# Keys as three products, values first, and a first load in slices, in a two-layer cross-attention and feed-forward kernel

## The chip, the cores and the metric

One core of one Trainium2 chip. The metric is the device time of one execution in microseconds, lower is better. The kernel keeps all five engines at work: TensorE (PE, matmuls), VectorE (DVE), ScalarE (ACT), GpSimd (POOL) and SyncE (SP, which issues the DMAs here). Each runs its own list of instructions in the written order; semaphores hold an instruction until others are done.

## The reference, cut to what matters

`x` has 2 x 256 rows of 512, `ctx_4096` 2 x 512 rows of 512. Everything is float32 at the boundary.

```python
x = x + xattn0(layernorm(x), ctx)     # 8-bit fake quantisation of both, then q1 @ q2
x = x + ffn0(layernorm(x))            # weights to fp4, rows to fp6, per block of 32; silu(gate) * up, down
x = x + xattn1(layernorm(x), ctx)     # 32 query heads, 8 key/value heads of 128, rope, softmax, wo
x = x + ffn1(layernorm(x))            # ternary weights with scales, inner width 1376
```

In `xattn1` the keys are `ctx @ wk` and the values `ctx @ wv`, both 1024 x 1024. They depend on the context alone, so they can be computed at any time before it. The change is about when and how they are computed.

## The kernel before

**Stages.** Stage one, 0 to about 122 us, does several things at once: the first layernorm and the quantised attention `xattn0`; the quantisation to fp4 and transposition of the weights of `ffn0` (8 chunks of four 128x512 tiles and a last single tile); and the projection of values and keys for `xattn1`. Stage two, 122 to 177 us, is `ffn0` for four tiles of 128 rows. Then follow `xattn1`, a loop over 32 heads (to about 600 us), and `ffn1`.

**Units.** A unit is one PSUM bank of 128x512: `("v", i, h)` is context tile i (0 to 7) times half h of `wv`; `("k", i, b)` is key head i for batch b. A float32 unit is four slices of the contraction, which the profile shows as eight matmuls. `STEPS` (line 40) gives for each of the eight steps the units before and after the first half of the chunk's transposes; five key units (`LATE_KEYS`) are worked off in stage two. Units rotate over banks 5, 6, 7; `take` waits until ScalarE has copied out the unit three places earlier. The sums of `xattn0` (in steps 3 and 4) and the transposes of q1 use the same banks.

**A weight chunk.** `mx_peaks` (VectorE, block maxima, 1339) and `mx_exponents` (two tensor_scalars, 1345 and 1347, giving `mx_e` and `mx_r`); `scale_in` (GpSimd, 1104); `mx_lift` (ScalarE, two halves, 882); `mx_round` (VectorE, 1357, 1360); `mx_clip` (VectorE, 1365); `scale_out` (GpSimd, 1110, giving `mx_w`); `mx_turn` (TensorE, two times eight transposes, 514); `mx_keep` (ScalarE, 874). The lists of all engines are written out by hand, two chunks apart: GpSimd does scale_in(i+2), then scale_out(i). `fp6_out` (GpSimd, 1115) is the last part of the quantisation of rows; VectorE's part of it is `fp6` and `fp6_clip` (1370 to 1382): a reduction, four small tensor_scalars, a multiply, a small tensor_scalar and a clip.

**Keys of head 0.** They don't go to the scratch memory as they are: ScalarE's `swap` copies them and their halves exchanged, GpSimd's `key_rotate` does three 128x512 tensor_tensors (rope), and SyncE stores the result. This is done for both batches near the start, from 27 and 41 us.

**SyncE's order.** wk of head 0, context columns of batch 0 (1 MB), x (1 MB), scalars, wv half 0, weight chunks 0 and 1, identity, context columns of batch 1, rope table, wv half 1, chunk 2, and so on. `three` (lines 663 to 665), used by the later stages, computes one product of operands that are split in a high and a low part (float32r) as high x high + high x low + low x high.

## Time and profile before

| | us |
|---|---|
| median of 3 runs | 702.56 (700.72 to 702.59) |
| the profiled execution | 702.53 |
| its span in the trace | 700.7 |
| TensorE busy | 668.3 (95%) |
| VectorE busy | 520.0 (74%) |
| GpSimd busy | 463.3 (66%) |
| ScalarE busy | 363.3 (52%) |

A timeline row gives start and length in us from the span's start, the engine, the line, what is written from what, and in brackets how long the engine sat idle before it and who ended that. A row of the chain says what the execution was waiting for at that time, followed back from the last instruction; `issue` is time in which the engine at hand waited for nothing that the profile shows. Matmul lengths include the tail of the last one, so back-to-back groups overlap by a little.

### The profile page before, as it was taken

The numbers are of one execution on the slowest core, as the hardware profiler recorded it, in microseconds if no ns is written. First come the engines' busy times: TensorE is split into PE (matmuls) and PEld (weight loads), VectorE is DVE, ScalarE is ACT, GpSimd is POOL, SyncE is SP. The second block draws the span as 40 slices with busy tenths as digits, with TensorE's granted clock in tenths as the row PEclk, the third lists the DMA queues.
The fourth block names the chain that finished last, engine by engine and source line by source line (L and its number), as shares of the span: only waits on it lengthen the run. The fifth ranks groups of instructions, "written<-read, shape, count | busy, mean of one in ns | idle before, by whom it ended". The sixth has DMA issues, their size and how long they took to land.

```text
span 700.7 us, 11095 instructions
## 1 busy us (share of the span) xinstructions
PE 668.3 (95%) x3152; PEld 494.0 (70%) x3152; DVE 520.0 (74%) x1046; ACT 363.3 (52%) x686; POOL 463.3 (66%) x407
## 2 busy tenths in 40 slices
PE   6999998899899999999999999999999999799997
PEld 2444443444577788888888888888888877688885
DVE  4999798777668888888888888888888886721122
ACT  2697434533565665666666665665665663211110
POOL 0697426432479878778789788688698478066661
PEclk9999999999999999999999999999999999999999
DMA  9985422140323132141131221221223012013311
GB/s 340 343 293 183 134 87 80 36 155 6 127 71 119 30 106 76 30 134 45 55 110 45 82 83 45 90 75 46 89 75 135 17 31 66 25 46 101 113 56 61
DMA packets 39420, 67.27 MB, mean 96 GB/s; under 512 B 3680, under 2 KB 12000, under 8 KB 38368
## 3 DMA queue, kind: packets, MB, share of 16 engines
q1 hardware_dynamic: 39392, 66.93, 28.9%
q8 instruction: 14, 0.23, 0.1%
q14 instruction: 14, 0.11, 0.1%
HBM read 57.48 MB, written 9.44 MB: 95 GB/s over the span
## 4 chain that ended last, share of the span: by engine, by line
PE 71%; POOL 10%; DVE 8%; issue 7%; ACT 2%; DMA 1%; SPq 0%; POOLq 0%; DVEq 0%; ACTq 0%
PE ps L663 16%; PE ps L665 16%; PE ps L664 16%; PE ps L731 11%; PE ps L696 7%; POOL mx_raw L1104 3%; POOL mx_w L1110 3%; PE ps L584 2%; PE ps L520 1%; DMA X<-in_x 1%; PE ps L536 1%; POOL prob L1161 1%; PE ps L620 1%; DVE mx_amax L1339 1%; DVE stats L1260 1%
## 5 line engine op out<-in xcount | busy, mean ns | idle before, releaser
L1009 ACT ACTIVATE prob<-ps,nmax 128x512 f32<-128x512 f32 x128 | 88.3, 690 | 97.4 <-DVE nmax L1487 97.0
L1161 POOL TENSOR_SCALAR prob<-prob,rinv 128x512 f32<-128x512 f32 x128 | 89.4, 698 | 73.7 <-DVE rinv L1494 73.6
L731 PE MATMUL ps<-xt,wq_sb 128*128 128x512 f32 x384 | 103.2, 393 | 3.8 <-DVE q_cos L1502 2.1
L1020 ACT CAST pT<-ps 128x512 fp32r<-128x512 f32 x128 | 75.1, 587 | 52.8 <-PE ps L696 51.9
L1487 DVE CUSTOM_DVE_ANT_0 ps<-ps,mask_sb 128x512 f32<-128x512 f32 x128 | 87.9, 687 | 6.7 <-PE ps L665 6.3
L1508 DVE TENSOR_TENSOR pT<-ps,pT 128x512 fp32r<-128x512 f32 x128 | 86.3, 674 | 3.0 <-ACT pT L1020 2.0
L731 PEld LDWEIGHTS ps<-xt,wq_sb 128*128 128x128 f32 x384 | 71.6, 188 | 22.0 <-issue 4.6
L696 PE MATMUL ps<-idf,prob 128*128 128x128 f32 x512 | 76.7, 272 | 0.4 <-POOL prob L1161 0.3
L696 PEld LDWEIGHTS ps<-idf,prob 128*128 128x128 f32 x512 | 63.8, 141 | 17.3 <-POOL prob L1161 1.6
L520 PE MATMUL ps<-ctxT,wk_sb 128*128 128x512 f32 x128 | 60.5, 613 | 6.5 <-DMA ctxT<-in_ctx_cols 6.5
L1104 POOL TENSOR_TENSOR mx_raw<-mx_raw,mx_r 128x2048 f32<-128x2048 f32 (+1 forms) x9 | 30.2, 3354 | 53.7 <-DVE mx_r L1347 53.7
L663 PE MATMUL ps<-pT,vt 128*128 128x512 f32 x128 | 61.1, 478 | 0.5 <-DVE pT L1508 0.5
L536 PE MATMUL ps<-wv_sb,ctxT 128*128 128x512 f32 x128 | 57.3, 597 | 0.6 <-ACT v_st L869 0.4
L1164 POOL TENSOR_TENSOR q_swp<-q_swp,ropeQ 128x512 f32<-128x512 f32 x32 | 47.0, 1469 | 10.9 <-ACT q_swp L1030 10.9
L663 PE MATMUL ps<-wo_sb,oT 128*128 128x512 f32 x128 | 50.3, 393 | 1.4 <-DVE X L1543 0.9
L663 PE MATMUL ps<-kt,qt 128*128 128x512 f32 x128 | 50.6, 395 | 0.9 <-DVE kt L1521 0.5
L1561 DVE SCALAR_TENSOR_TENSOR int<-ps,sc,silu 128x512 f32<-128x512 f32 x11 | 8.3, 750 | 57.6 <-PE ps L665 57.6
L665 PE MATMUL ps<-pT,vt 128*128 128x512 f32 x128 | 50.8, 397 | 0.0
L664 PE MATMUL ps<-pT,vt 128*128 128x512 f32 x128 | 50.3, 393 | 0.0
L665 PE MATMUL ps<-kt,qt 128*128 128x512 f32 x128 | 50.1, 392 | 0.0
L1145 POOL TENSOR_TENSOR wo_sb<-wo_raw,wo_sb 128x512 fp32r<-128x512 f32 x32 | 48.3, 1511 | 2.7
L664 PE MATMUL ps<-wo_sb,oT 128*128 128x512 f32 x128 | 50.0, 391 | 0.0
(177 smaller groups left out, 1587.9 us busy)
## 6 DMA issues: line engine op xcount, KB each, us to landing
mx_raw<-in_mxw SPq DMA_DIRECT2D x8, 1024.0 KB, 5.5
wq_raw<-in_wq SPq DMA_DIRECT2D x32, 256.0 KB, 3.2
wo_raw<-in_wo SPq DMA_DIRECT2D x32, 256.0 KB, 2.7
v_scr<-v_st SPq DMA_DIRECT2D x16, 256.0 KB, 2.5
kr<-k_scr SPq DMA_DIRECT2D x16, 256.0 KB, 2.9
vr<-v_scr SPq DMA_DIRECT2D x16, 256.0 KB, 3.4
k_scr<-k_st SPq DMA_DIRECT2D x14, 256.0 KB, 2.1
kr_swp<-k_scr SPq DMA_DIRECT2D x28, 128.0 KB, 3.3
```

The source lines that it names most:

```text
L520: last = mm(bank(n), wk_sb[:, i % 2, k], ctxT[:, k, b * CTX:(b + 1) * CTX], start=(k == 0), stop=(k == KD - 1))
L536: last = mm(bank(n), ctxT[:, k, i * P:(i + 1) * P], wv_sb[:, k, h * 512:(h + 1) * 512], start=(k == 0), stop=(k == KD - 1))
L663: mm(out_ap, left[0], right[0], start=first, stop=False)
L664: mm(out_ap, left[0], right[1], start=False, stop=False)
L665: return mm(out_ap, left[1], right[0], start=False, stop=final)
L696: last = nc.tensor.transpose(bank(2 + i % 2)[:, k * P:(k + 1) * P], prob[:, i, k * P:(k + 1) * P], idf[:])
L731: last = mm(query_bank(H), wq_sb[:, par, l, k], xt[:, r, k], start=(n == 0), stop=(n == 11))
L1009: nc.scalar.activation(prob[:, j], bank(j % 2), ACT.Exp, bias=nmax[:, j:j + 1], scale=-1.0, accum_out=rsum[:, j:j + 1]).then_inc(exps, 1)
L1020: copy(pT[:, v % 2, 0, :, i * P:(i + 1) * P], bank(2 + i % 2).rearrange("p (k c) -> p k c", k=4)).then_inc(ph_ready, 1)
L1161: nc.gpsimd.tensor_scalar(prob[:, i], prob[:, i], rinv[:, i:i + 1], 1.0, ALU.mult, ALU.mult).then_inc(probs, 1)
L1487: nc.vector.tensor_tensor_reduce(out=bank(j % 2), in0=bank(j % 2), in1=mask_sb[:, 2 * (u % 2) + j % 2], scale=-1.0, scalar=BIG, op0=ALU.ad ...
L1508: tt(pT[:, v % 2, 1, :, i * P:(i + 1) * P], bank(2 + i % 2).rearrange("p (k c) -> p k c", k=4), pT[:, v % 2, 0, :, i * P:(i + 1) * P].bitc ...
```

## The change

Values come first and keys last in stage one. The first four value units run together, slice by slice, on banks 0, 5, 6 and 7, as the slices of context and wv (256 KB each) arrive; two pairs of slices are loaded ahead of x and two behind it, all ahead of the first weight chunk. Keys are computed with `three`: context and key weights are split in a high part (ScalarE's copy to float32r: `context_high`, `weights_high`) and a low part (GpSimd's subtraction: `context_low`, `weights_low`). The high part of the context overwrites wv, the low part overwrites the context, so both wait for the value units that read them. Key weights have four slots; slots 2 and 3 lie in the staging buffer of the values, and their loads wait for the value stores. Head 0 is third among the key heads, so `key_rotate` moves to the ends of GpSimd's steps 5 and 6. `mx_r` moves from VectorE to GpSimd (`exponents`). ScalarE's first instructions are reordered. The buffers of the attention stage and of the last net are laid out in another order, with the same sizes.

```diff
...
 STEPS = (
-    ([("v", 0, 0), ("v", 1, 0), ("v", 2, 0), ("v", 3, 0)], [("k", 0, 1)]),
-    ([("v", 0, 1), ("v", 1, 1), ("k", 1, 0)], [("k", 1, 1)]),
-    ([("v", 2, 1), ("k", 2, 0)], [("v", 3, 1)]),
-    ([("k", 2, 1), ("v", 4, 0)], [("v", 4, 1)]),
-    ([("k", 3, 0), ("k", 3, 1)], [("v", 5, 0)]),
-    ([("v", 5, 1), ("k", 4, 0)], [("k", 4, 1)]),
-    ([("v", 6, 0), ("v", 6, 1)], [("v", 7, 0)]),
-    ([("v", 7, 1), ("k", 5, 0)], []),
+    ([("v", 0, 0), ("v", 1, 0), ("v", 2, 0), ("v", 3, 0)], [("v", 4, 0)]),
+    ([("v", 5, 0), ("v", 6, 0), ("v", 7, 0)], [("v", 0, 1)]),
+    ([("v", 1, 1), ("v", 2, 1)], [("v", 3, 1)]),
+    ([("v", 4, 1), ("v", 5, 1)], [("v", 6, 1)]),
+    ([("v", 7, 1), ("k", 1, 0)], [("k", 2, 0)]),
+    ([("k", 1, 1), ("k", 2, 1)], [("k", 0, 0)]),
+    ([("k", 0, 1), ("k", 3, 0)], [("k", 3, 1)]),
+    ([("k", 4, 0), ("k", 4, 1), ("k", 5, 0)], []),
 )
 LATE_KEYS = ((5, 1), (6, 0), (6, 1), (7, 0), (7, 1))
 LATE_BANK = (3, 6, 2, 1, 3)
 VALUES = [unit[1:] for step in STEPS for part in step for unit in part if unit[0] == "v"]
-KEYS_AT = {1: 2, 2: 3, 4: 4, 5: 5}
+KEYS = [unit[1:] for step in STEPS for part in step for unit in part if unit[0] == "k"] + list(LATE_KEYS)
+STORED_KEYS = [key for key in KEYS if key[0] > 0]
+HEADS = [head for head, batch in KEYS if batch == 0]
 Q_AT, L0_AT = 1, 4
+V_LAST = 4
+
+HIGH_AT = {V_LAST - 1: (0, 1), V_LAST: (2, 3), V_LAST + 1: (4, 5), V_LAST + 2: (6,)}
...
         for i in range(NFULL):
-            rotation += STEPS[i][0] + STEPS[i][1]
+            rotation += STEPS[i][0][1 if i == 0 else 0:] + STEPS[i][1]
...
 
+            if unit == ("v", 0, 0):
+                return 0
...
+        def wk_parts(i):
+
+            turn = HEADS.index(i)
+            raw, high, low = (wk_01, wk_hi01, wk_lo01) if turn % 4 < 2 else (wk_23, wk_hi23, wk_lo23)
+            return raw[:, turn % 2], high[:, turn % 2], low[:, turn % 2]
...
             def k_load(i):
 
-                after(sp, k_sums, 2 * (i - 1))
-                sp.dma_start(wk_sb[:, i % 2], wk[i]).then_inc(wk_in[i % 2], 16)
+                turn = HEADS.index(i)
+                if turn >= 4:
+                    sp.wait_ge(*keys_summed(HEADS[turn - 4], 1))
+                sp.dma_start(wk_parts(i)[0], wk[i]).then_inc(wk_in[turn % 4], 16)
 
...
+            def slice_load(k):
+                sp.dma_start(ctxT[:, k, 0:CTX], ctx_cols[k * P:(k + 1) * P, 0:CTX]).then_inc(ctxT0_in[k], 16)
+                sp.dma_start(wv_sb[:, k, 0:512], wv[k * P:(k + 1) * P, 0:512]).then_inc(wv0_in[k], 16)
...
-            k_load(0)
-            ctxT_load(0)
+            slice_load(0)
+            slice_load(1)
             sp.dma_start(X[:], x.rearrange("(t p) d -> p t d", p=P)).then_inc(x_in, 16)
             sp.dma_start(sc[:], scalars).then_inc(sc_in, 16)
-            wv_load(0)
+            slice_load(2)
+            slice_load(3)
             mx_load(0)
             mx_load(1)
             sp.dma_start(idf[:], ident).then_inc(id_in, 16)
-            ctxT_load(1)
-            sp.dma_start(ropeK[:], rope_k).then_inc(rk_in, 16)
-            wv_load(1)
+            sp.dma_start(ctxT[:, :, CTX:CTOK], ctx_cols[:, CTX:CTOK].rearrange("(k p) c -> p k c", p=P)).then_inc(ctxT1_in, 16)
             mx_load(2)
-            k_load(1)
             ctx_load(0)
+            sp.dma_start(wv_sb[:, :, 512:1024], wv[:, 512:1024].rearrange("(k p) c -> p k c", p=P)).then_inc(wv1_in, 16)
             stores(STEPS[0][0])
             mx_load(NRAW)
             ctx_load(1)
+            k_load(HEADS[0])
+            k_load(HEADS[1])
+            sp.dma_start(ropeK[:], rope_k).then_inc(rk_in, 16)
+            stores(STEPS[0][1])
             for i in range(1, NFULL):
-                if i in KEYS_AT:
-                    k_load(KEYS_AT[i])
                 if i + NRAW <= NFULL:
                     mx_load(i + NRAW)
-                if i == 1:
-                    for b in range(2):
-                        sp.wait_ge(k_roped, b + 1)
-                        sp.dma_start(k_scr[0, b], k_own[:, b]).then_inc(k0_stored, 16)
-                stores(STEPS[i][0] + STEPS[i][1])
-            k_load(6)
+                if i > V_LAST:
+                    k_load(HEADS[4 if i == V_LAST + 1 else i])
+                if i == V_LAST + 1:
+                    k_load(HEADS[5])
+                units = [unit for part in STEPS[i] for unit in part if unit[:2] != ("k", 0)]
+                if i == V_LAST:
+                    stores(units[:1])
+                    for slot in range(NSLOT):
+                        sp.wait_ge(v_stored[slot], 16 * 2 * NCT // NSLOT)
+                    k_load(HEADS[2])
+                    k_load(HEADS[3])
+                    units = units[1:]
+                stores(units)
+            for b in range(2):
+                sp.wait_ge(k_roped, b + 1)
+                sp.dma_start(k_scr[0, b], k_own[:, b]).then_inc(k0_stored, 16)
 
...
+            def three(out_ap, left, right, first, final):
+
+                mm(out_ap, left[0], right[0], start=first, stop=False)
+                mm(out_ap, left[0], right[1], start=False, stop=False)
+                return mm(out_ap, left[1], right[0], start=False, stop=final)
+
             def key_part(i, b, n, parts):
+                pe.wait_ge(wk_split, HEADS.index(i) + 1)
+                _, high, low = wk_parts(i)
+                cols = slice(b * CTX, (b + 1) * CTX)
                 for k in parts:
-                    last = mm(bank(n), wk_sb[:, i % 2, k], ctxT[:, k, b * CTX:(b + 1) * CTX], start=(k == 0), stop=(k == KD - 1))
+                    if i == HEADS[0] and k % 2 == 0:
+                        pe.wait_ge(ctx_split, 2 * b + k // 2 + 1)
+                    last = three(bank(n), [high[:, k], low[:, k]], [ctx_hi[:, k, cols], ctx_lo[:, k, cols]], k == 0, k == KD - 1)
...
+            def first_values():
+
+                units = STEPS[0][0]
+                for k in range(KD):
+                    pe.wait_ge(ctxT0_in[k], 16)
+                    pe.wait_ge(wv0_in[k], 16)
+                    for unit in units:
+                        i = unit[1]
+                        last = mm(bank(rotating(unit)), ctxT[:, k, i * P:(i + 1) * P], wv_sb[:, k, 0:512], start=(k == 0), stop=(k == KD - 1))
+                        if k == KD - 1:
+                            last.then_inc(v_sums, 1)
...
-            keys(0, 0, 0)
+            first_values()
             for i in range(NFULL):
-                project_context(STEPS[i][0])
+                if i > 0:
+                    project_context(STEPS[i][0])
                 if i == 1:
                     pe.wait_ge(consts_ready, 2)
-                    pe.wait_ge(*keys_out(0, 0))
+                    pe.wait_ge(v_copied, 1)
                 if 0 < i < NFULL - 1:
...
             def swap(b):
 
-                act.wait_ge(k_sums, b + 1)
+                act.wait_ge(*keys_summed(0, b))
...
             def copy_unit(unit):
                 kind, i, j = unit
-                if kind == "k":
+                if kind == "k" and i == 0:
+                    swap(j)
+                elif kind == "k":
                     copy_keys(i, j)
                 else:
                     copy_values(i, j)
 
-            swap(0)
+            def context_high(b):
+
+                act.wait_ge(v_sums, NCT * (b + 1))
+                cols = slice(b * CTX, (b + 1) * CTX)
+                for k in range(0, KD, 2):
+                    copy(ctx_hi[:, k:k + 2, cols], ctxT[:, k:k + 2, cols]).then_inc(ctx_high, 1)
+
+            def weights_high(i):
+                raw, high, _ = wk_parts(i)
+                turn = HEADS.index(i)
+                act.wait_ge(wk_in[turn % 4], 16 * (turn // 4 + 1))
+                copy(high, raw).then_inc(wk_high, 1)
+
+            rows_scale()
+            mx_lift(0, 0)
+            mx_lift(0, 1)
             copy_values(0, 0)
             copy_values(1, 0)
-            mx_lift(0, 0)
-            mx_lift(0, 1)
-            rows_scale()
-            copy_values(2, 0)
             act.wait_ge(id_in, 16)
             copy(idb[:], idf[:]).then_inc(consts_ready, 1)
             mx_lift(1, 0)
+            copy_values(2, 0)
+            mx_lift(1, 1)
             copy_values(3, 0)
-            mx_lift(1, 1)
-            swap(1)
             rows_keep()
+            copy_values(4, 0)
             for i in range(1, NFULL):
                 copy_unit(STEPS[i][0][0])
+                if i == V_LAST:
+                    context_high(1)
                 mx_lift(i + 1, 0)
                 if i == 1:
                     copy_unit(STEPS[i][0][1])
@@ -948,6 +1017,11 @@
                 if i == Q_AT:
                     keep_quantised(0)
                     context_scale(1)
+                if i == V_LAST - 2:
+                    context_high(0)
+                for turn in HIGH_AT.get(i, ()):
+                    weights_high(HEADS[turn])
+            weights_high(HEADS[7])
             keep_quantised(1)
...
+            def exponents(i):
+                n, p = width(i) // BLK, i % NRAW
+                pool.wait_ge(mx_expo, i + 1)
+                ts(mx_r[:, p, 0:n].bitcast(I32), mx_e[:, p, 0:n].bitcast(I32), -1.0, -(2.0 ** 24), ALU.mult, ALU.add).then_inc(mx_scale, 1)
+
             def scale_in(i):
+                exponents(i)
...
+            def context_low(b):
+
+                if b == 0:
+                    pool.wait_ge(v_sums, VALUES.index((3, 1)) + 1)
+                cols = slice(b * CTX, (b + 1) * CTX)
+                for k in range(0, KD, 2):
+                    pool.wait_ge(ctx_high, 2 * b + k // 2 + 1)
+                    tt(ctx_lo[:, k:k + 2, cols], ctxT[:, k:k + 2, cols], ctx_hi[:, k:k + 2, cols].bitcast(F32), ALU.subtract).then_inc(ctx_split, 1)
+
+            def weights_low(i):
+                raw, high, low = wk_parts(i)
+                pool.wait_ge(wk_high, HEADS.index(i) + 1)
+                tt(low, raw, high.bitcast(F32), ALU.subtract).then_inc(wk_split, 1)
+
             scale_in(0)
             scale_in(1)
-            key_rotate(0)
-
             for i in range(NFULL):
                 if i + 2 <= NFULL:
                     scale_in(i + 2)
                 if i == L0_AT + 2:
                     fp6_out(q1[:].rearrange("p t d -> p (t d)"), NT * D, 0, q1_ready)
                 scale_out(i)
-                if i == 0:
-                    key_rotate(1)
+                if i == V_LAST - 2:
+                    context_low(0)
+                for turn in HIGH_AT.get(i, ()):
+                    weights_low(HEADS[turn])
+                if i == V_LAST - 1:
+                    context_low(1)
+                if i in (V_LAST + 1, V_LAST + 2):
+                    key_rotate(i - V_LAST - 1)
+            weights_low(HEADS[7])
             scale_out(NFULL)
...
+            pool.wait_ge(k0_stored, 32)
             for t in range(NT):
...
             def mx_exponents(i):
                 p, m = i % NRAW, width(i) // BLK
                 after(dve, mx_ready, i - NRAW + 1)
-                dve.wait_ge(mxa_step, 2 * i + 1)
-                ts(mx_e[:, p, 0:m].bitcast(U32), mx_amax[:, 0:m].bitcast(U32), EXP_MASK, 0x80000000, ALU.bitwise_and, ALU.bitwise_or).then_inc(mxa_step, 1)
-                dve.wait_ge(mxa_step, 2 * i + 2)
-                ts(mx_r[:, p, 0:m].bitcast(I32), mx_e[:, p, 0:m].bitcast(I32), -1.0, -(2.0 ** 24), ALU.mult, ALU.add).then_inc(mx_scale, 1)
+                dve.wait_ge(mx_peak, i + 1)
+                ts(mx_e[:, p, 0:m].bitcast(U32), mx_amax[:, 0:m].bitcast(U32), EXP_MASK, 0x80000000, ALU.bitwise_and, ALU.bitwise_or).then_inc(mx_expo, 1)
...
```

## Rows read from the trace of the kernel before

**Rows 1.** The page, busy time of the engines: us (share of span), instructions.
```profile
...
PE 668.3 (95%) x3152; PEld 494.0 (70%) x3152; DVE 520.0 (74%) x1046; ACT 363.3 (52%) x686; POOL 463.3 (66%) x407
...
```

**Rows 2.** The chain of waits in order of time: start us, length us, what.
```profile
...
86.99 13.49 issue
...
100.51 3.64 POOL mx_raw L1104
...
104.15 3.60 POOL mx_w L1110
...
107.80 0.62 PE ps L514 x8
...
```

**Rows 3.** TensorE's timeline: start, length, what xcount [idle before it, and its releaser].
```profile
...
6.45 5.71 PE L520 MATMUL ps<-ctxT,wk_sb 128*128 128x512 f32 x8 [6.45 <-DMA ctxT<-in_ctx_cols]
...
12.29 14.00 PE L536 MATMUL ps<-wv_sb,ctxT 128*128 128x512 f32 x32
...
71.55 1.03 PE L499 MATMUL ps<-q,ones 128*128 128x512 bf16 x4
...
107.80 0.62 PE L514 MATMUL ps<-idb,mx_w 128*128 128x128 bf16 x8 [1.49 <-POOL mx_w L1110]
...
119.12 1.06 PE L490 MATMUL ps<-idb,q 128*128 128x128 bf16 x16
...
121.79 4.93 PE L584 MATMUL ps<-WT,q1T 128*128 128x512 bf16 x24 [1.62 <-ACT q1T L839]
...
177.07 5.71 PE L731 MATMUL ps<-xt,wq_sb 128*128 128x512 f32 x24 [1.16 <-DVE xt L1456]
...
```

**Rows 4.** VectorE's timeline, the same columns.
```profile
...
9.52 2.47 DVE L1260 BATCH_NORM_STATS2 stats<-X 128x6 f32<-128x512 f32 x4 [9.52 <-DMA X<-in_x]
...
22.10 1.54 DVE L1345 TENSOR_SCALAR mx_e<-mx_amax 128x64 uint32<-128x64 uint32 x1
...
41.61 1.26 DVE L1345 TENSOR_SCALAR mx_e<-mx_amax 128x64 uint32<-128x64 uint32 x1
...
42.91 1.19 DVE L1347 TENSOR_SCALAR mx_r<-mx_e 128x64 int32<-128x64 int32 x1
...
108.03 0.20 DVE L1371 TENSOR_SCALAR f_amax<-f_amax 128x64 f32<-128x64 f32 x1
...
108.95 2.29 DVE L1375 TENSOR_TENSOR f<-xhat,f_r 128x2048 fp8e4<-128x2048 f32 x1
...
111.38 1.22 DVE L1382 TENSOR_SCALAR f6c<-f 128x2048 bf16<-128x2048 fp8e4 x1
...
129.52 0.68 DVE L1371 TENSOR_SCALAR f_amax<-f_amax 128x44 f32<-128x44 f32 x1
...
136.94 0.56 DVE L1424 TENSOR_TENSOR int<-silu,ps 128x384 f32<-128x384 f32 x1 [2.21 <-ACT silu L958]
...
```

**Rows 5.** ScalarE's groups to 180 us: xcount | busy us, mean ns of one | idle.
```profile
...
L882 ACT ACTIVATE ps<-mx_raw 128x1024 f32<-128x1024 f32 x16 | 16.4, 1030 | 4.3 <-POOL mx_raw L1104 4.3
...
L869 ACT COPY v_st<-ps 128x512 f32<-128x512 f32 x16 | 9.3, 582 | 21.7 <-PE ps L536 21.7
...
```

**Rows 6.** The first key matmuls (line 520), shortest/median/longest duration.
```profile
...
L520 PE MATMUL ps<-ctxT,wk_sb x16: 592/593/1193, 6.5 to 29.1; 128*128 128x512 f32 x16
...
```

**Rows 7.** GpSimd's groups, mean ns of one.
```profile
...
L1145 POOL TENSOR_TENSOR wo_sb<-wo_raw,wo_sb 128x512 fp32r<-128x512 f32 x32 | 48.3, 1511 | 2.7
...
L1225 POOL TENSOR_TENSOR fw_even<-ffn_raw,fw_even 128x1024 fp32r<-128x1024 f32 x5 | 11.9, 2387 | 1.4 <-DVE int1s L1563 1.0
...
L1222 POOL TENSOR_SCALAR fw_even<-ffn_raw 128x512 fp32r<-128x512 f32 x10 | 6.1, 627 | 21.0 <-issue 21.0
...
```

**Rows 8.** GpSimd's timeline.
```profile
...
19.95 3.64 POOL L1104 TENSOR_TENSOR mx_raw<-mx_raw,mx_r 128x2048 f32<-128x2048 f32 x1 [18.99 <-DVE mx_r L1347]
...
41.10 1.72 POOL L1122 TENSOR_TENSOR k_swp<-k_swp,ropeK 128x512 f32<-128x512 f32 x1
...
42.78 1.27 POOL L1123 TENSOR_TENSOR k_own<-k_own,ropeK 128x512 f32<-128x512 f32 x1
...
104.12 3.63 POOL L1110 TENSOR_TENSOR mx_w<-mx_q,mx_e 128x2048 bf16<-128x2048 bf16 x1
...
113.58 1.05 POOL L1104 TENSOR_TENSOR mx_raw<-mx_raw,mx_r 128x512 f32<-128x512 f32 x1 [5.83 <-DVE mx_r L1347]
...
114.58 3.64 POOL L1115 TENSOR_TENSOR q<-f6c,f_e 128x2048 bf16<-128x2048 bf16 x1
...
129.11 1.05 POOL L1110 TENSOR_TENSOR mx_w<-mx_q,mx_e 128x512 bf16<-128x512 bf16 x1 [2.18 <-PE ps L514]
...
```

84 lines of the change are left out of this document (41 added, 43 removed).

## The prediction

> **What bounds the kernel now.** The page comes first: TensorE is busy 95% of the span and GpSimd 66% [rows 1]. That invites "fewer TensorE passes, less time". The chain of waits, read in order of time over the stretch that the change rewrites, says otherwise: from 17 us to 108 us it runs from one GpSimd tensor_tensor to the next, each of 3.64 us, with `issue` pieces between (up to 13.49 us, where GpSimd waits for VectorE's scale), and TensorE enters only at 107.80, after a wait of 1.49 us for GpSimd's `mx_w` [rows 2, 3]. TensorE, VectorE and GpSimd are all close to the limit in this stage, coupled through buffers. So the timelines of the engines must be read side by side, not the busy shares. Behind 121.79 (first gate/up matmul) the same three engines pass the rows of the first feed-forward net around; from 177.07 (first query) the attention loop and the last net follow, which the change leaves as they are.
>
> The views are differenced at two marks: 121.79 and 177.07 [rows 3]. I walked the four written orders and SyncE's forward with the durations of the rows, releasing each instruction when its last wait is met. The present orders, walked so, give 120.4 and 175.0, that is 1.4 and 2.0 us early; the new ones are compared with these, mark by mark, and only differences are used. The sum goes on the profiled execution, 702.53 us (span 700.7 and 1.8 around it), which is the median of the runs (702.56) but for 0.03.
>
> **Start.** Before, key weights and a whole context half (1.25 MB) land at 6.45, and 2.25 MB, with x, at 9.52: 3.07 us per MB [rows 3, 4]. The first pair of slices (0.5 MB) lands by that rate at 6.45 - 0.75 x 3.07 = 4.2; x, now behind 1 MB instead of 1.25, 0.8 earlier at 8.7. The other two pairs follow by 12, before TensorE wants them. First values: 16 slices of work in 4 x 3.44 us (a unit: 14.00/4 less its tail) plus 2.3 us, because the first eight matmuls took 5.71 instead of 3.44: 4.2 + 16.1 = 20.3. Nothing is gained by that: all four units end together and fill banks 0, 5, 6, 7, and v(4,0) needs bank 5. ScalarE now has rows_scale, lift(0,0) and lift(0,1) ahead of the copies. scale_in(0) is done at 16.3 (peaks) + 2.3 + 0.2 + 0.3 (exponents on GpSimd) + 3.64 = 22.7, two lifts and two copies follow, 0.95 and 0.48 each (their 1.03 and 0.58 less the 0.1 by which the next one overlaps) [rows 5]: 25.6. TensorE idles 5.3 us from 20.3.
>
> What that idleness does to its clock: the first matmul, after 6.45 us without work, shows 1193 ns against 592 of the later ones, the lower of the two levels, 1.2 against 2.4 GHz (the column of the granted clock reads 1.00 all the same); after the longest later waits here, 1.6 us, nothing of the sort is seen [rows 3, 6]. 5.3 is nearer to 6.45, so I take the slow start again: 2.2 us on TensorE, between 0 and 2.3. "TensorE: Matmul & The Clock Gate" of the Trainium skill (Part 1, the clock gate) states that an idle engine falls back to half rate; by it the 1.0 us below is owed, without it not.
>
> **26 to 98 us.** At the first attention sums (71.55) TensorE used to have 16 units done, now 15: -2.2 (start) - 3.4 (a unit fewer) + 5.3 (idle) + 2.2 (clock), less what the old waits took: the walk has +0.3. A key unit as three products: 12 matmuls; 24 of that kind take 5.71 us, so 0.23 each and 2.78 per unit instead of 3.44: 0.66 saved, 11 units in the stage 7.3 us, 5 late ones 3.3 us [rows 3]. The additions: ScalarE copies the context's high part in four pieces (0.95 each, as a lift) and eight weight slices (0.52 each, a copy), 8 us, in idle time of 2 to 5 us per step. GpSimd gets four 128x1024 subtractions at 2.39 (9.6 us), eight 128x512 at 1.27 (10.2 us; 1.27 is the rotation's step) and nine exponent operations [rows 7, 8]. No row has a 64-column GpSimd operation of this kind. It lies between 0 and 0.63, the tensor_scalar of 512 columns. Two-source operations of 512 and 2048 columns take 1.05 and 3.64, 1.7 ns per column, and a one-source one I take at half of that: 0.63 - 448 x 0.00085 = 0.25, 2.2 us in all. GpSimd idles 2 us per step early and 13.5 us before 100.51 [rows 2], so 22 us seem to fit.
>
> **The lock.** They don't, for a reason that the timelines show. A VectorE tensor_scalar of 64 columns takes 0.20 us, but 1.54 at 22.10, 1.26 at 41.61, 1.19 at 42.91, 0.68 at 129.52. Each such one ends when the GpSimd operation then running ends: 23.60 against 23.64; 42.82 against 42.87; 44.06 against 44.10; 130.16 against 130.20. Where GpSimd is idle (108.03) it takes 0.20. GpSimd waits in turn: 1.72 instead of 1.27 at 41.10 behind VectorE's clip. Two in a row are each held, since GpSimd's next operation slips in between them [rows 4, 8]. Tensor_reduce and operations with a PSUM source run through unhurt. In the walk a VectorE tensor_scalar from SBUF waits for the running GpSimd operation, and the other way round; this reproduces the present VectorE timeline within 0.5 us up to 65 us. So each added GpSimd operation costs VectorE as much as GpSimd. "GPSIMD Engine Reference" of the Trainium skill (Key points) adds VectorE instructions with two SBUF inputs to those in contention; the 2.29 us multiply of the quantisation (two SBUF inputs) would then be held too, by up to 1.3 us once or twice: 1 to 2 us above my sum. No row here has it beside GpSimd work.
>
> What the products save up to here: l(1) can start 1 us earlier than before, but exponent(6) on VectorE is held by the context subtraction (2.4 us), so the sums are read at the same time, and scale 7 comes with +0.1 (warm clock) or +1.1 (slow start). TensorE's saved time (2 + 5 key units) turns into waiting before the transposes at 107.80: 5.7 us instead of 1.49.
>
> **98 to 122 us.** Behind scale_out(5) (ends 107.75) GpSimd now has two weight subtractions and key_rotate(0), 2 x 1.27 + 3 x 1.27 = 6.3 us, where it had idled till 113.58. Beside them VectorE runs the layernorm output's quantisation: reduce to 108.0, four small tensor_scalars (0.9 us with gaps), the multiply, the clip; done just before chunk 8's scale, which GpSimd gets at 113.58 [rows 4, 8]. Now each of the four is held behind one of the five GpSimd operations: 4 x 1.27 + 0.9 = 6.0 instead of 0.9, +5.0. Then exponents(8), scale_in(8), the 3.64 us product q1, the transposes: +5.0 again, less 0.9 by which TensorE had been the later one at 119.12 (q1 was ready at 114.58 + 3.64 = 118.22): first gate/up +4.2 (warm), +5.3 (slow start).
>
> **122 to 177 us.** Behind q1 GpSimd has scale_out(6) 3.64, a subtraction, key_rotate(1) 3.8, scale_out(7) 3.64, a subtraction, scale_out(8) 1.05: 14.7 us without a pause. VectorE's clips of chunks 7 and 8 are held (+0.6 and +1.2), as is the last rounding by the queue, so its first product comes +6.0; its small tensor_scalars at 129.52 ff. are held by scale_out(7), the last subtraction and scale_out(8): +3.7 more. Of these 2.2 us are lost time it had anyway before 136.94 [rows 4]; chunk 7's transposes come +6.5, in front of gate_up(1). The second quantised tile is +8.6, and from there the loop goes as before, +8.1 at the last transposes of `int_q`. Seven quarters of late key units (1.15 us) then stand on TensorE's way to the last row transposes: +7.0 at the first query (warm), +8.1 (slow start). The late key that is spread over units -2 and -1 saves 0.66, half of it before a wait of 0.46: -0.3. SyncE's key loads wait for sums that come in time; its x, wq and key loads behind the last transposes move with them. Later stages: 0. Sum: 702.5 + 8.0 - 0.3 = 710.2 us.
>
> **Rivals.** (1) The clock stays up through the 5.3 us: 702.5 + 7.0 - 0.3 = 709.2. For: the column reads 1.00. Against: the first matmul. It is inside the forecast's own range. (2) No price of the lock, the other side: if VectorE's small operations fell between GpSimd's (another phase by 1 us at 108 and 130), the walk without holding gives -1.5 at 177.07: TensorE's late keys pay, the stage does not, and 702.5 - 1.5 - 0.3 = 700.7 to 701.5. It decides from the point where the four small tensor_scalars at 108 us take under 1 us. Against it: GpSimd is then busy without gaps for 6 us. Half the holding gives 704 to 706. (3) GpSimd's subtractions take 1.51 us as the `wo` ones do beside VectorE [rows 7]: each 0.24 dearer, the walk gives +2.3: 712.5; with exponent operations of 0.6 us, +0.9 more: 713.4. (4) The change doesn't do what it says: the key units run at 3.44 (weight loads not hidden): +1.5, since only the late ones are on the way: 711.7.
>
> **Chances.** Forecast with (1): 0.60, own range 707.5 to 712; (2) fully 0.13, half 0.12; (3) and (4) together 0.15. The range that leaves out no more than 2 in 10: 702.5 to 713.5. A measurement tells 0.3% (2.1 us) from no change, so same is 700.5 to 704.6: faster 0.09 (the lower half of rival 2 and errors of the walk), same 0.13, slower 0.78.
>
> **What would show it.** Right: TensorE starts near 4.2, idles some 5 us before v(4,0), matmuls at double length after it; a wait of 5 to 6 us ahead of the transposes near 107; four small tensor_scalars near 108 of over 1 us each; the first gate/up at about 126 to 127, the first query at 184 to 186. Wrong: VectorE's small operations at 0.2 us beside GpSimd work, or GpSimd idle between 108 and 138; then the time is near 701. If the first query comes near 177 and the total is off all the same, the moved buffers of the attention stage did it, which I priced at nothing.

## The result, and the profile after

| | before | after |
|---|---|---|
| median of the runs | 702.58 (700.72 to 702.89, 4 runs) | 712.03 (711.31 to 712.56, 4 runs) |
| the profiled execution, its span | 702.53, 700.7 | 711.55, 709.8 |

The ratio is 1.0139, 95% interval 1.0119 to 1.0160: the change costs 9.45 us. The forecast was 710.2, its own range 707.5 to 712, which the measured 712.03 misses by 0.03; the wide range was 702.5 to 713.5.

On the page TensorE is busy for 4.6 us less than in [rows 1], VectorE for 14.3 and GpSimd for 27.5 more:

```profile
...
PE 663.7 (94%) x3211; PEld 508.5 (72%) x3216; DVE 534.3 (75%) x1037; ACT 371.9 (52%) x698; POOL 490.8 (69%) x428
...
```

VectorE has nine instructions fewer, and yet works longer. TensorE's timeline (against [rows 3]; columns as there) shows how late each mark is:

```profile
...
4.64 15.68 PE L589 MATMUL ps<-wv_sb,ctxT 128*128 128x512 f32 x32 [4.64 <-DMA wv_sb<-in_wv]
...
27.65 12.71 PE L599 MATMUL ps<-wv_sb,ctxT 128*128 128x512 f32 x24 [7.32 <-ACT v_st L924]
...
92.03 0.50 PE L566 MATMUL ps<-ctx_hi,wk_hi 128*128 128x512 f32 x1 [3.27 <-DVE col L1423]
...
113.91 1.03 PE L560 MATMUL ps<-idb,mx_w 128*128 128x128 bf16 x8 [5.21 <-POOL mx_w L1190]
...
131.75 6.21 PE L648 MATMUL ps<-WT,q1T 128*128 128x512 bf16 x24 [1.57 <-ACT q1T L896]
...
188.36 5.72 PE L788 MATMUL ps<-xt,wq_sb 128*128 128x512 f32 x24 [1.17 <-DVE xt L1555]
...
```

The transposes of chunk 5 come 6.1 us later (113.91 against 107.80) behind a wait of 5.21 instead of 1.49, the first gate/up 10.0 later, the first query 11.3. From there on nothing is added: the last result of VectorE is 10.8 late. The span ends only 9.1 later, since the last output transfers took 2.5 us behind it in this execution and 4.2 in that of the kernel before. This end comes in two lengths: 2.4 to 2.6 us in eleven of the fourteen traces, 4.2 to 4.6 in three (before, before_extra, keys_whole). So totals of single executions can differ by 1.7 to 2 us for nothing, and the experiments are also compared at VectorE's last result.

VectorE's timeline (against [rows 4]) shows where its 14.3 us are. Between 84 and 123 us it has no gap:

```profile
...
56.55 1.22 DVE L1456 SCALAR_TENSOR_TENSOR mx_raw<-ps,mx_raw 128x1024 f32<-128x1024 bf16 x1 [3.33 <-ACT ps L937]
...
61.34 2.28 DVE L1440 TENSOR_REDUCE mx_amax<-mx_raw 128x64 f32<-128x2048 f32 x1
...
64.66 2.85 DVE L1464 TENSOR_SCALAR mx_q<-mx_q 128x2048 bf16<-128x2048 bf16 x1
67.43 2.34 DVE L1446 TENSOR_SCALAR mx_e<-mx_amax 128x64 uint32<-128x64 uint32 x1
...
93.46 2.91 DVE L1430 SCALAR_TENSOR_TENSOR X<-xhat,sx,X 128x512 f32<-128x512 f32 x2
...
106.01 0.18 DVE L1446 TENSOR_SCALAR mx_e<-mx_amax 128x64 uint32<-128x64 uint32 x1
...
113.80 0.20 DVE L1470 TENSOR_SCALAR f_amax<-f_amax 128x64 f32<-128x64 f32 x1
114.03 1.15 DVE L1471 TENSOR_SCALAR f_amax<-f_amax 128x64 uint32<-128x64 uint32 x1
115.21 1.20 DVE L1472 TENSOR_SCALAR f_r<-f_amax 128x64 int32<-128x64 int32 x1
116.44 1.20 DVE L1473 TENSOR_SCALAR f_r<-f_r 128x64 f32<-128x64 f32 x1
117.68 3.32 DVE L1474 TENSOR_TENSOR f<-xhat,f_r 128x2048 fp8e4<-128x2048 f32 x1
...
```

GpSimd in the same stretch (against [rows 8]):

```profile
...
106.28 0.24 POOL L1178 TENSOR_SCALAR mx_r<-mx_e 128x64 int32<-128x64 int32 x1 [8.77 <-DVE mx_e L1446]
...
113.82 2.54 POOL L1220 TENSOR_TENSOR wk_lo<-wk,wk_hi 128x512 fp32r<-128x512 f32 x2
116.32 1.27 POOL L1202 TENSOR_TENSOR k_swp<-k_swp,ropeK 128x512 f32<-128x512 f32 x1
117.56 1.29 POOL L1203 TENSOR_TENSOR k_own<-k_own,ropeK 128x512 f32<-128x512 f32 x1
118.99 3.16 POOL L1206 TENSOR_TENSOR k_own<-k_own,k_swp 128x512 f32<-128x512 f32 x1
...
```

To be seen: the exponents (64 columns) take 0.18 us at 106.01, where GpSimd is idle, and 2.34 at 67.43, beside a subtraction. The first small instruction starts at 113.80, 0.02 us ahead of GpSimd's subtraction, and takes its 0.20; each of the next three ends within 0.1 us of a GpSimd operation (115.09, 116.36, 117.59). GpSimd waits in turn: its addition at 118.99 takes 3.16 instead of 1.27; the product begun at 117.68 is out at 121.00, and the addition 1.15 later. The row at 61.34 is a mark ahead of the first subtraction (63.66); the kernel before reaches it at 59.58, so 1.8 us of the delay are there already, behind the wait of 3.33 us for ScalarE.

### The profile page after: what moved, and what is told of

It is laid out like the page before. It is cut to its first block, busy times and chain, and to the rows that moved or that the text cites. A ratio compares the mean times of both kernels' runs of the same rounds, so it can differ in the third digit from the quotient of the medians.

```text
span 709.8 us, 11262 instructions
## 1 busy us (share of the span) xinstructions
PE 663.7 (94%) x3211; PEld 508.5 (72%) x3216; DVE 534.3 (75%) x1037; ACT 371.9 (52%) x698; POOL 490.8 (69%) x428
## 4 chain that ended last, share of the span: by engine, by line
PE 69%; DVE 15%; POOL 5%; issue 5%; ACT 3%; DMA 2%; SPq 0%; POOLq 0%; DVEq 0%; ACTq 0%
PE ps L566 16%; PE ps L568 16%; PE ps L567 15%; PE ps L788 11%; PE ps L753 7%; PE ps L648 2%; DVE mx_amax L1440 2%; DVE mx_raw L1456 1%; DVE f L1474 1%; DMA X<-in_x 1%; POOL mx_raw L1184 1%; DMA v_scr<-v_st 1%; DVE f_amax L1469 1%; PE ps L599 1%; DVE stats L1360 1%
## 5 line engine op out<-in xcount | busy, mean ns | idle before, releaser
L599 PE MATMUL ps<-wv_sb,ctxT 128*128 128x512 f32 x96 | 44.9, 620 | 7.3 <-ACT v_st L924 7.3
L566 PE MATMUL ps<-wo_sb,oT 128*128 128x512 f32 x128 | 50.2, 393 | 1.4 <-DVE X L1642 0.9
L566 PE MATMUL ps<-kt,qt 128*128 128x512 f32 x128 | 50.1, 392 | 0.9 <-DVE kt L1620 0.5
L568 PE MATMUL ps<-kt,qt 128*128 128x512 f32 x128 | 50.2, 392 | 0.0
L567 PE MATMUL ps<-wo_sb,oT 128*128 128x512 f32 x128 | 50.0, 391 | 0.0
L568 PE MATMUL ps<-wo_sb,oT 128*128 128x512 f32 x128 | 50.0, 390 | 0.0
L567 PE MATMUL ps<-kt,qt 128*128 128x512 f32 x128 | 49.9, 390 | 0.0
```

The source lines that it names most:

```text
L566: mm(out_ap, left[0], right[0], start=first, stop=False)
L567: mm(out_ap, left[0], right[1], start=False, stop=False)
L568: return mm(out_ap, left[1], right[0], start=False, stop=final)
L599: last = mm(bank(n), ctxT[:, k, i * P:(i + 1) * P], wv_sb[:, k, h * 512:(h + 1) * 512], start=(k == 0), stop=(k == KD - 1))
```

## The experiments

Times are medians; the ratio is to the kernel before on the same chip, with its 95% interval. The marks are of the profiled execution: the exponents of chunk 7 (VectorE), the end of the FP6 chain's last instruction (`f6c`), the first gate/up and the first query (TensorE), and the end of VectorE's last result.

Two things limit what the differences say. The experiments ran on three chips, where the median of the kernel before was 702.46 (no_lows, rotate_late, keys_whole, before_extra), 702.44 (start, norm_late, before_six, before_fp6_first) and 701.16 (no_early_lows, no_late_lows, keep_busy, before_early_last); the changed kernel was not run again beside them. And kernels whose orders are the same up to there reach VectorE's reduction of chunk 4 at anything from 47.95 (keep_busy) to 49.61 (norm_late), 48.84 in the changed kernel, so that a mark further on which moved by less than 1.7 us need not have been moved by the edit.

| kernel | us | ratio | expon. 7 | `f6c` ends | gate/up | query | last result |
|---|---|---|---|---|---|---|---|
| before | 702.5 | | 100.02 | 112.60 | 121.79 | 177.07 | 696.47 |
| after | 712.03 | 1.0119 to 1.0160 | 106.01 | 123.34 | 131.75 | 188.36 | 707.26 |
| no_lows | 705.77 | 1.0036 to 1.0069 | 101.26 | 116.53 | 126.94 | 182.10 | 701.08 |
| no_early_lows | 708.13 | 1.0066 to 1.0124 | 100.83 | 118.16 | 126.56 | 183.14 | 703.64 |
| no_late_lows | 709.92 | 1.0093 to 1.0143 | 106.33 | 121.61 | 131.32 | 186.49 | 705.56 |
| keys_whole | 708.23 | 1.0065 to 1.0119 | 102.14 | 117.39 | 127.46 | 182.73 | 701.73 |
| rotate_late | 718.12 | 1.0203 to 1.0257 | 106.23 | 120.55 | 130.93 | 195.07 | 713.75 |
| start | 711.86 | 1.0106 to 1.0165 | 105.02 | 122.36 | 130.78 | 187.43 | 707.60 |
| norm_late | 717.08 | 1.0181 to 1.0236 | 99.90 | 128.84 | 138.14 | 194.07 | 712.73 |
| keep_busy | 711.56 | 1.0116 to 1.0167 | 105.18 | 122.53 | 130.94 | 187.76 | 706.49 |
| before_extra | 706.52 | 1.0040 to 1.0082 | 102.46 | 116.95 | 125.62 | 181.25 | 700.83 |
| before_six | 707.78 | 1.0047 to 1.0109 | 100.13 | 115.75 | 124.06 | 180.87 | 700.70 |
| before_fp6_first | 703.46 | 0.9999 to 1.0037 | 99.76 | 112.35 | 122.16 | 177.44 | 696.87 |
| before_early_last | 702.26 | 0.9993 to 1.0020 | 99.99 | 113.58 | 121.77 | 177.04 | 696.42 |

### Without GpSimd's subtractions (no_lows)

```diff
...
-    last = three(bank(n), [high[:, k], low[:, k]], [ctx_hi[:, k, cols], ctx_lo[:, k, cols]], ...)
+    last = three(bank(n), [high[:, k], high[:, k]], [ctx_hi[:, k, cols], ctx_hi[:, k, cols]], ...)
...
-    context_low(0), context_low(1), weights_low(...)   # GpSimd
```

> Leaves out GpSimd's twelve subtractions (four of context_low, eight of weights_low); the key products take the rounded part in place of the difference, so TensorE, VectorE and ScalarE have the same instructions as in the changed kernel, and the keys are less exact. Theory A (VectorE and GpSimd hold one another: every subtraction that runs beside a VectorE tensor_scalar, or a VectorE instruction with both inputs in SBUF, lengthens it): the clips, exponents and the four small ones of the FP6 chain fall back to 0.68, 0.18 and 0.20 us, the mark 'first gate/up' (131.75 in the changed kernel) falls to 124 to 126, and the time to 703 to 706 us. Rival B (the loss is the late start and TensorE's fallen clock, GpSimd's additions fit into its idle time): the time stays at 711 to 712 us.

The time falls by 6.3 us (by 6.2 at VectorE's last result), the exponents of chunk 7 come 4.75 sooner. VectorE's list of instructions is the same; its timeline, where the subtraction of the context stood:

```profile
...
64.73 0.69 DVE L1457 TENSOR_SCALAR mx_q<-mx_q 128x2048 bf16<-128x2048 bf16 x1
65.33 0.19 DVE L1439 TENSOR_SCALAR mx_e<-mx_amax 128x64 uint32<-128x64 uint32 x1
...
77.06 1.42 DVE L1423 SCALAR_TENSOR_TENSOR X<-xhat,sx,X 128x512 f32<-128x512 f32 x2
...
109.27 1.14 DVE L1464 TENSOR_SCALAR f_amax<-f_amax 128x64 uint32<-128x64 uint32 x1
...
```

Theory A holds in the total and here: clip 0.69 instead of 2.85, exponents 0.19 instead of 2.34, X 1.42 instead of 2.67. In the FP6 chain it expected too much: two of the four small ones stay at 1.14 and 1.20 and the product at 3.25, now held by the rotation, which moved up into the place of the subtractions; so the first gate/up comes at 126.94 and not by 126. 3.3 us of the loss remain (4.6 at the last result).

### The early and the late half apart (no_early_lows, no_late_lows)

```diff
-    last = three(..., [high[:, k], low[:, k]], [ctx_hi[:, k, cols], ctx_lo[:, k, cols]], ...)
+    # no_early_lows: low = high for the first four heads, ctx_hi for ctx_lo, their subtractions out
+    # no_late_lows: low = high for the last four heads, their subtractions out
```

> Leaves out the eight subtractions that stand before 98 us (four of the context, weight slices of the first four heads; the rounded part is used in their place), keeps the four of the last weight slices. It tests the step of the forecast that took the stretch from 26 to 98 us at nothing. Theory A (they cost through VectorE, as its clips, exponents and the updates of X are held at 2.3 to 2.9 us): the exponents of chunk 7, at 106.01 in the changed kernel, come at 101.3 as without any subtraction, the first gate/up at 127 to 128, 706 to 708 us. Rival B (the four beside the FP6 chain carry the loss): 711 us.

> Leaves out the other four subtractions, those of the weight slices of the last four heads (two of them beside the FP6 chain at 113.8), and keeps the eight before 98 us. Theory A: the exponents of chunk 7 stay at 106.0, the chain after it gets 1 to 2 us shorter, because the rotations behind move up into the place of what is left out, and hold the same instructions; 709.5 to 711 us. Rival B (these four carry the loss): 706 to 707 us.

Without the eight before 98 us the exponents of chunk 7 come at 100.83, 5.2 us sooner, and the time falls by 3.9. Without the four late ones that mark doesn't move (106.33), `f6c` ends 1.7 sooner, the query comes 1.9 sooner, and the time falls by 2.1. Both are as theory A had it but for 0.1 us (708.13 for 706 to 708) and 0.4 at the first gate/up (126.56 for 127 to 128), and together 6.0 of the 6.3. These differences are taken across chips; by the ratios the two are worth 3.1 and 1.5 us of 6.1, at VectorE's last result 3.6 and 1.7 of 6.2, and no_late_lows alone is not clear of noise (its interval overlaps that of the changed kernel). The order of the two holds by every measure: the stretch that the forecast took at nothing has the larger part.

### The keys whole again (keys_whole)

```diff
-    last = three(bank(n), [high[:, k], low[:, k]], [ctx_hi[:, k, cols], ctx_lo[:, k, cols]], ...)
+    last = mm(bank(n), raw[:, k], ctxT[:, k, cols], start=(k == 0), stop=(k == KD - 1))
-    context_high, weights_high (ScalarE), context_low, weights_low (GpSimd)
```

> Undoes one part: values first and the slices ahead of x stay, but keys are one float32 product per part again, from the unrounded context and weight slices; no rounding on ScalarE and no subtraction on GpSimd. A key unit is 3.44 instead of 2.78 us, 16 units cost TensorE 10.6 us more. Theory A: GpSimd's holding goes (8 us), part of the 10.6 us falls into waits of TensorE for VectorE and GpSimd that are there anyway (3.3 and 5.2 us in the stage); 704 to 707 us. Rival B (the three products are where a gain is, the order is where the loss is): 711 + 10.6 less what the waits take in, 714 to 720 us.

708.23. It is outside both, 1.2 above A's range and 5.8 below B's, and says the same as A: dropping the splits repays 3.8 us, though TensorE has 10.6 more to do. Against no_lows it is 2.5 us slower in the median, but the profiled execution has the long end (4.6 us behind the last result for 2.5): up to VectorE's last result it is 0.65 later, to the first query 0.63. So the cheaper units, with ScalarE's rounding that they need, are worth 0.6 to 2.5 us here, not 10.6. The rest of the change without them (keys_whole against before: order, start, the exponents on GpSimd, the moved buffers) costs 5.8, or 5.3 at the last result.

### The rotations moved back (rotate_late)

```diff
                 scale_out(i)
 ...
-                if i in (V_LAST + 1, V_LAST + 2):
-                    key_rotate(i - V_LAST - 1)
             weights_low(HEADS[7])
             scale_out(NFULL)
+            key_rotate(0)
+            key_rotate(1)
```

> Same work as the changed kernel, but head 0's two rotations (six multiplications and additions of GpSimd) stand behind the last scale_out instead of in rounds 5 and 6, where they run beside the FP6 chain of VectorE. Theory A: in the FP6 chain the three small tensor_scalar at 1.15 to 1.20 us, the product at 3.32 and the exponent at 1.17 fall to 0.2, 2.3 and 0.2 or nearly (one 1.27 us subtraction of a weight slice is still beside them), so the first gate/up comes 3 to 5 us sooner, and the time is 707 to 709 us. Rival B: nothing that TensorE waits for moves, 711 to 712 us. Rival C (whatever is moved is paid later: the rotations stand before the first FP6 product of the first layer's network, about 143 us): the first gate/up sooner, the first query not, 711 us.

Slower by 6.1 us than the changed kernel, 9 above the range of theory A and 7 above rival C. The FP6 chain got shorter by 2.8 us (`f6c` at 120.55; the product at 2.29 again). But the first gate/up came only 0.8 sooner, as TensorE now came to q's transposes (127.75) with its own work, and the first query 6.7 later. Rival C had the place and not the size. GpSimd's timeline shows it:

```profile
...
144.82 2.64 POOL L1202 TENSOR_TENSOR k_swp<-k_swp,ropeK 128x512 f32<-128x512 f32 x1
147.43 2.00 POOL L1203 TENSOR_TENSOR k_own<-k_own,ropeK 128x512 f32<-128x512 f32 x1
149.91 1.26 POOL L1206 TENSOR_TENSOR k_own<-k_own,k_swp 128x512 f32<-128x512 f32 x1 [0.49 <-POOL k_own L1203]
153.32 2.56 POOL L1195 TENSOR_TENSOR int_q<-f6c,f_e 128x1408 bf16<-128x1408 bf16 x1 [2.15 <-DMA k_scr<-k_own]
...
```

The six run beside the next FP6 chain, that of the first layer's network, and it holds them too. The first `int_q` then waits another 2.15 us for the transfer of the rotated keys, whose memory it takes over, and TensorE 3.90 for `int_q`.

### The start mended (start)

```diff
+            copy(early[:], ones[:, 0:8])
             rows_scale()
-            mx_lift(0, 0)
-            mx_lift(0, 1)
             copy_values(0, 0)
             copy_values(1, 0)
+            mx_lift(0, 0)
+            mx_lift(0, 1)
 ...
+            copy_values(2, 0)
             mx_lift(1, 0)
-            copy_values(2, 0)
+            copy_values(3, 0)
             mx_lift(1, 1)
-            copy_values(3, 0)
```

> The changed kernel with its start mended: ScalarE makes one small copy (128x8) before it waits for x, and copies the first four values out of their banks ahead of the four lifts of the first chunks. TensorE's wait of 7.32 us (until 27.65) is for the first of these copies. Theory A (the stage is set by VectorE, which is busy without a gap from 84 to 123 us): TensorE starts again at 20 to 23 us, 5 us sooner, but at 113.91 it waits for the same rounds of the low-bit weights, which come only 0 to 1 us sooner; 710.5 to 711.5 us. Rival B (the late start is carried to the end): 706 to 707 us. Rival C (the lifts come later by four copies, and with them every round): 713 us.

TensorE goes on at 23.04 instead of 27.65, the first gate/up comes 1.0 sooner, the time is 711.86: theory A, 0.4 above its range. The first row of ScalarE's timeline in the changed kernel is a table load, behind the wait for VectorE's scales; in this one it starts at 0.75 us, as before the change:

```profile
18.07 1.28 ACT L943 ACT_TABLE_LOAD   x1 [18.07 <-DVE sx L1404]
...
```

In the changed kernel it costs little as well: ScalarE still waits 1.13 us for GpSimd before its first lift at 24.62. 4.6 us won at the start are worth at most one, because TensorE just waits longer for chunk 5 (6.81 for 5.21), and even that one is not shown: the reduction of chunk 4 comes at 47.91, and in keep_busy, with the start unmended, at 47.95.

### The norm behind the clip (norm_late)

```diff
-                if i == L0_AT + 1:
-                    dve.wait_ge(l0_done, NT)
-                    layernorm()
 ...
                 mx_clip(i)
                 if i + 2 <= NFULL:
                     mx_exponents(i + 2)
+                if i == L0_AT + 1:
+                    dve.wait_ge(l0_done, NT)
+                    layernorm()
```

> The changed kernel with one thing moved in VectorE's order: in round 5 the clip of chunk 5 and the exponents of chunk 7 come before the layer norm (98.5 to 105.4 us) instead of behind it. TensorE's wait of 5.21 us before 113.91 and GpSimd's of 8.77 us before 106.28 are for these. Theory A (VectorE and GpSimd hold one another): the wait of TensorE goes, but GpSimd's work (3.6 + 3.6 us and 4 to 6 of subtractions and rotation) now stands beside the norm's chain of eleven instructions of 0.16 us, each with all inputs in SBUF; it takes 6 to 10 us longer, the FP6 chain runs free, and the first gate/up comes at 129 to 134 us; 709 to 714 us. Rival B (no holding, order alone): the wait and the rotations' overlap go, the first gate/up 4 to 5 us sooner, 706.5 to 708 us.

717.08, 3 us above the range of theory A, 9 above B's; the gate/up is 4 behind A's range. It is the clearest picture of the holding. The timelines of VectorE, GpSimd and TensorE in this kernel:

```profile
...
102.91 1.26 DVE L1375 TENSOR_SCALAR var_eps<-meanvar 128x4 f32<-128x4 f32 x1
104.21 3.57 DVE L1376 TENSOR_SCALAR rstd<-var_eps 128x4 int32<-128x4 int32 x1
107.82 1.20 DVE L1378 SCALAR_TENSOR_TENSOR newton<-rstd 128x4 f32<-128x4 f32 x1
109.05 1.21 DVE L1379 TENSOR_TENSOR newton<-newton,var_eps 128x4 f32<-128x4 f32 x1
...
```

```profile
...
104.11 3.65 POOL L1190 TENSOR_TENSOR mx_w<-mx_q,mx_e 128x2048 bf16<-128x2048 bf16 x1
107.71 2.53 POOL L1220 TENSOR_TENSOR wk_lo<-wk,wk_hi 128x512 fp32r<-128x512 f32 x2
110.20 1.29 POOL L1202 TENSOR_TENSOR k_swp<-k_swp,ropeK 128x512 f32<-128x512 f32 x1
...
```

```profile
...
107.82 0.62 PE L560 MATMUL ps<-idb,mx_w 128*128 128x128 bf16 x8
...
123.66 1.01 PE L560 MATMUL ps<-idb,mx_w 128*128 128x128 bf16 x8 [12.41 <-ACT WT L929]
...
```

An instruction on four columns, 0.17 us alone, takes 3.57 and ends (107.78) with the operation beside it (107.76). The chain of eleven, 2.2 us in the changed kernel, takes 11.8, 9.6 more, which is in the expected 6 to 10; the FP6 chain behind it runs free (its small ones 0.20 each, from 124.27). TensorE's wait before the first transposes of chunk 5 is gone (107.82), but VectorE's rounds of chunk 7 stand behind the norm and come at 116.58 instead of 106.11. ScalarE waits for them, its copy that frees the bank stands behind that, and TensorE waits 12.41 us before the second transposes.

### TensorE kept busy (keep_busy)

```diff
+            def keep_busy(kept, count):
+                pe.wait_ge(mx_kept, kept)
+                for _ in range(count):
+                    mm(bank(0), ctx_hi[:, 0, 0:P], ctx_hi[:, 0, 0:CTX], start=True, stop=True)
 ...
+                if i == L0_AT + 1:
+                    keep_busy(2 * L0_AT, 14)
 ...
+                if i == L0_AT + 2:
+                    keep_busy(2 * L0_AT + 2, 22)
```

> The changed kernel with 36 idle matmuls (128x512, 0.23 us each, into the bank of the low-bit turns) in TensorE's two waits: 14 in the one of 3.27 us before 92.03, and 22 in the one of 5.21 us before 113.91. Nothing reads them. In the changed kernel the granted clock falls to half behind both waits for 3 to 4 us each. Theory A (the clock falls because TensorE had been idle, and it costs about 1.5 us a time, of which VectorE's chain takes most): no spacing of 0.43 us behind them, the first gate/up 0 to 1.5 us sooner, 710.5 to 711.7 us. Rival B (the clock falls for another cause): the 0.43 us stay. Rival C (TensorE's late keys are the path, so all of it counts): 709 us.

In windows of 2 us (us, busy time of TensorE, weight loads, VectorE, ScalarE, GpSimd; granted clock; DMA share, GB/s), the changed kernel first, then this one:

```profile
94.00:96.00 2.00, 2.00 (x6) 1.57 (x5) 2.00 (x2) 0.00 (x0) 2.00 (x3) 0.50 0.00 0
114.00:116.00 2.00, 2.00 (x11) 1.81 (x12) 1.94 (x2) 1.01 (x1) 2.00 (x2) 0.50 0.00 0
...
```

```profile
94.00:96.00 2.00, 2.00 (x10) 1.60 (x10) 2.00 (x2) 1.52 (x2) 2.00 (x2) 1.00 0.29 78
114.00:116.00 2.00, 2.00 (x10) 1.61 (x10) 1.93 (x3) 0.76 (x1) 2.00 (x3) 1.00 0.00 0
...
```

The half clock behind the two waits is gone, so idleness had caused it. The first gate/up comes 0.8 sooner, but not for that: VectorE's reduction of chunk 4, long before the first idle matmul (87.53), is 0.9 sooner already. The changed kernel, then this one:

```profile
48.84 2.27 DVE L1440 TENSOR_REDUCE mx_amax<-mx_raw 128x64 f32<-128x2048 f32 x1
```

```profile
47.95 2.28 DVE L1450 TENSOR_REDUCE mx_amax<-mx_raw 128x64 f32<-128x2048 f32 x1
```

And TensorE, ahead now, waits 2.90 before q's transposes instead of 1.29, and the clock falls there: the first 24 gate/up matmuls take 7.55 instead of 6.21 us (4.93 in [rows 3]). 711.56 against 712.03 can't be told from nothing.

### GpSimd operations added to the kernel before (before_extra, before_six)

```diff
+                if i == 2:
+                    context_extra(0)     # before_extra: twelve idle subtractions in the changed kernel's places
 ...
+                if i in (L0_AT + 1, L0_AT + 2):
+                    rotation_extra()     # before_six: three idle 128x512 multiplications, twice
```

> The kernel before, with twelve idle-work subtractions added on GpSimd, of the shapes (128x1024 and 128x512) and in the rounds where the changed kernel has its own; nothing reads their results. TensorE, ScalarE and VectorE have the instructions of the kernel before. Theory A: VectorE's tensor_scalars beside them go from 0.2 and 0.7 to 1 to 3 us as in the changed kernel; the first gate/up, at 121.79 before, comes 4 to 8 us later; 706 to 711 us. Rival B (the additions fit into GpSimd's idle time, 116 us of waits before 130): 702.6 us, within 0.5.

> The kernel before with six idle multiplications 128x512 added on GpSimd, three each behind the scale_out of rounds 5 and 6, which is where the changed kernel rotates head 0's keys (before, these stand at the start). Nothing reads their results. Theory A: the moved rotations are the part of the loss that stays when the subtractions are left out (3.3 us): the small tensor_scalar of the FP6 chain at 108 us are held at 1.2 us each and its product at 2.3 becomes 3.3, the first gate/up 2.5 to 4 us later, 705 to 706.5 us. Rival B (that rest is the start's): 702.5 us, within 0.5.

before_extra: +4.1 us (4.4 at the last result), in theory A's range; the gate/up 3.8 later, just under it. The kernel before had no room for this work, though GpSimd idled a third of the time. before_six: `f6c` 3.15 later, the first gate/up 2.3, the first query 3.8, since the clock fell at 124; the four runs spread from 705.1 to 709.1, so its +5.3, above the range, is known to 2 us only, and the profiled one (705.08) is the lowest; at VectorE's last result it is 4.2 later. VectorE's rows of before_six, against 0.20 each in [rows 4]:

```profile
...
108.15 1.00 DVE L1382 TENSOR_SCALAR f_amax<-f_amax 128x64 f32<-128x64 f32 x1
109.18 1.31 DVE L1383 TENSOR_SCALAR f_amax<-f_amax 128x64 uint32<-128x64 uint32 x1
110.53 1.31 DVE L1384 TENSOR_SCALAR f_r<-f_amax 128x64 int32<-128x64 int32 x1
111.87 0.20 DVE L1385 TENSOR_SCALAR f_r<-f_r 128x64 f32<-128x64 f32 x1
...
```

Six operations of this length in this place cost as much as no_lows leaves (3.3 us); that these are what it leaves is not shown by that.

### Two attempts at a faster kernel (before_fp6_first, before_early_last)

```diff
+                if i == L0_AT + 2:
+                    fp6_out(q1[:]..., NT * D, 0, q1_ready)     # before_fp6_first: ahead of scale_in
                 if i + 2 <= NFULL:
                     scale_in(i + 2)
 ...
+                if last_chunk:
+                    mx_exponents(NFULL)     # before_early_last: behind the FP6 chain's first reduction
```

> The kernel before with GpSimd's order in round 6 turned round: the FP6 product of the first layer norm (q) ahead of the scaling of the last chunk. It waits at 112.60 for f6c, but starts only at 114.58, behind the last chunk's 1.05 us that came in at 113.58. Theory A (this product is on the path to the first gate/up): it starts at 112.7, the first gate/up 1.5 to 2 us sooner, and all after it: 700.5 to 701.1 us. Rival B (the last chunk's scaling, now 3.6 us later, is late for its lift and turn): 702.5 or more.

> The kernel before with one instruction of VectorE moved: the exponents of the last chunk (two tensor_scalar of 0.2 us) right behind the first reduction of the FP6 chain, at 108 us, instead of behind it all at 113.4. The last chunk's scaling (1.05 us on GpSimd) then runs at 108.3, and the FP6 product q starts when f6c is there (112.6) instead of at 114.58; and no exponents stand beside q, which took the gain when the product alone was put first (they took 3.61 us). Theory A: the small tensor_scalars beside the scaling wait 0.8 us in all, q starts at 113.4, the first gate/up comes at 120 to 120.8 instead of 121.8; 700.9 to 701.8 us. Rival B (the first gate/up waits for the rounds of chunk 7, not for q): 702.5 us.

Neither is faster than before (703.46 against 702.44, 702.26 against 701.16, both intervals with 1 in them). In the first, q starts at 112.43 instead of 114.58, and holds the exponents of the last chunk (0.17 us in the kernel before), so that the rounds behind come 3.2 us later, 116.59 for 113.41. VectorE's row:

```profile
...
112.86 3.61 DVE L1345 TENSOR_SCALAR mx_e<-mx_amax 128x16 uint32<-128x16 uint32 x1
...
```

In the second this is avoided, q ends 0.5 us sooner, and the first gate/up stands at 121.77. TensorE comes to q's transposes at 119.09 with its own work in either kernel (119.12 before), and q had been there since 118.22. Both expectations missed the row 119.12 of [rows 3].

## Why the forecast came out as it did

**The direction and the mechanism** were right, and named ahead: VectorE's tensor_scalars and GpSimd's operations hold one another, so GpSimd's idle time is no free room. Leaving the subtractions out, adding them to the kernel before, and the norm's chain of norm_late show it from three sides. The rule of "GPSIMD Engine Reference" of the Trainium skill (Key points), that VectorE instructions with two SBUF inputs contend too, is borne out by this trace: the FP6 product takes 3.32 us instead of 2.29, the updates of X 2.91 for two instead of 1.42.

**The signs.** As stated ahead: the start near 4.2 (4.64), half clock behind TensorE's idle time (7.32 us for the 5.3), a wait of 5 to 6 before chunk 5's transposes (5.21), small tensor_scalars of over 1 us (three of the four). Missed: the first gate/up, stated at 126 to 127, came at 131.75, the first query, at 184 to 186, at 188.36.

**Start.** The slices land at 4.64 (4.2 forecast). x lands at 10.41, not at 8.7: my rate of 3.07 us per MB was that of two large transfers, and between 4 and 8 us the slices moved at 222 to 292 GB/s, where before it was 351 to 389. TensorE waited 7.32 us for 5.3, for that: the first chunk is scaled at 24.59, where the working had 22.7. The table load of 1.28, which had moved behind the wait for VectorE's scales, is not on this path, as ScalarE waits 1.13 us for that scaling behind it. The half clock behind it, taken from one matmul at 1193 ns, was there: windows of 2 us from 26 to 32 show 0.50. The rule on the idle clock in "TensorE: Matmul & The Clock Gate" of the Trainium skill (Part 1, the clock gate) agrees. All this hardly counted: the start experiment gives back 4.6 of it for at most 1 us at the first gate/up and 0.2 in the total, neither of them clear of noise.

**26 to 98 us** is the step that failed. I put the scale of chunk 7 at +0.1 to +1.1, since "22 us seem to fit" into GpSimd's idle time; it was +6.0. no_early_lows puts 5.2 of it on the eight subtractions (4.8 when both are counted from the reduction of chunk 5, 61.34 and 60.97). 1.8 us are there before the first of them, at 61.34 for 59.58, behind ScalarE's lift; of these some 0.6 are made up again where nothing is subtracted (+1.2 at this mark in no_lows). I had the lock in hand, one paragraph later, and applied it to the exponents of chunk 6 alone. Two clips (2.85 and 2.41 for 0.69) and two exponents (2.34, 2.37 for 0.18) cost 8.2 us together, the updates of X another 2.7; VectorE's waits of before took in a part.

**98 to 131 us.** The size was right and its parts were not: +4.2 forecast on top of what came before (+5.3 less +1.1), +4.0 measured (+9.96 at the gate/up, +5.99 at the exponents). Held were three small ones and not four, 3.0 us; the product brought 1.0, `f_e` behind it 1.0. The product's 1.0 was not in my sum but named above it (up to 1.3 us, once or twice), and it stands in the place of the fourth small one.

**131 to 188 us.** +2.8 forecast (+8.1 less +5.3), +1.3 measured. The holding is less than in my walk: leaving out the last slices' subtractions (no_late_lows) takes 1.4 us from this leg. The clock, which fell before the first gate/up (6.21 us for 4.93), was not in my sum, so the holding itself is smaller still.

**The sum.** Forecast +7.7, measured +9.45. The first query is 3.2 us later than forecast (+11.3 for +8.1); 0.5 come back behind it (0.3 forecast), and the end of the span came 1.7 nearer in this pair of executions. So the total flatters the working, and that it came within 1.8 us is in part luck: the term for 26 to 98 us was 4.9 too small, that behind 131 us 1.5 too large, and the short end took 1.7 more. Of the rivals, (2), no price of the lock, is refuted by before_extra, where it expected 702.6 within 0.5; (4), dear products, by key matmuls 0.23 us apart; (1) by the half clock. (3), dearer subtractions, is not: beside VectorE's small ones two of them take 2.54 us (113.82), but the eight weight subtractions average 1.505 us, its very figure, and the four of the context 2.83 for 2.39, since VectorE holds them. Its 712.5 is also nearest to the time measured. What it had as a length of their own is the same lock from GpSimd's side, and no run tells the two sides apart. Its exponent operation of 0.6 us is refuted (0.24, for my 0.25).

**Left open.** How much of keys_whole's 5.8 us is the rotations' place and how much the order of the units was bounded (before_six, 2.3 at the gate/up) and not separated. Where the 1.8 us before 61.34 come from, and why x lands later, was not tried. A version with the subtractions where VectorE works from PSUM was not run.

## What to carry to other kernels

Before work is put into GpSimd's idle time, look at what VectorE does in the same microseconds: a chain of small tensor_scalars there pays for each GpSimd operation with that operation's whole length, and GpSimd with VectorE's. What the rows suggest, and no run here has tried, is to move such work beside instructions that read PSUM or reduce. When several orders are close to their limits, ask which one is without gaps (here VectorE from 84 to 123 us), because time won on another can go into a longer wait there (6.81 us for 5.21 in start).

## What the runs showed of the hardware

- A VectorE instruction of 0.16 to 0.20 us with its inputs in SBUF took 3.57 and 3.61 us beside GpSimd operations of 3.65 and 4.02, and ended within 0.05 us of them. In all fourteen traces the nine reductions of 2048 columns took 2.27 to 2.29 us, and the 32 halves of the rounding, which read PSUM and SBUF, 1.21 to 1.23, whatever ran beside them.
- TensorE's granted clock was at half after idle times of 7.32, 3.27 and 5.21 us, and stayed up after one of 1.62 in the kernel before (121.79). It also fell behind a wait of 1.57 where another had ended 2.6 us earlier (one of 1.29 in the changed kernel, of 2.02 in before_six), with q's transposes of 1.07 us between them, and behind a single one of 2.11 or 2.12 after the same transposes in four kernels (no_lows, no_late_lows, rotate_late, norm_late; 0.50 in the windows behind it). After one of 2.23 in before_fp6_first it stayed up (24 matmuls in 4.93 us). So the length of the wait alone doesn't tell.
- Idle matmuls in a wait kept the clock up behind it (keep_busy: 1.00 where it had been 0.50), and it fell at the next wait, of 2.90 us.
- The time from VectorE's last result to the end of the span was 2.4 to 2.6 us in eleven traces and 4.2 to 4.6 in three, behind the same four output transfers.
